# Spreading a mixture-of-experts kernel's indirect row DMAs over its expert rounds, one per step

## What is computed

```python
x = x + _L0_conv_ref(_ln_c(x), ...)       # kq, v, softmax(kq kq^T), out projection, per image of 256 points
t = _to_tokens(x)
t = t + _L0_ffn_ref(_ln_t(t), ...)
# _L0_ffn_ref, flat = the 2048 normalised tokens of 64 values
logits = flat @ router_w.T
topk_probs, topk_idx = jax.lax.top_k(jax.nn.softmax(logits, axis=-1), 2)     # of 8 experts
gates = ...                                # the two probabilities over their sum
h = silu(flat @ w1[e].T) * (flat @ w3[e].T)                                  # 682 values
out = sum over the token's two experts of gate * (h @ w2[e].T)
```

## Time and profile before

| | us |
|---|---|
| Median of 3 runs | 175.12 |
| Lowest, highest | 175.03, 176.37 |
| Span of the profiled execution, first to last instruction | 238.2 |
| PE, DVE, ACT, POOL busy in it | 166.9, 99.7, 70.8, 85.7 |

### The profile page before, as it was taken

The page is one execution under the profiler, slowest core; times in us unless marked ns, Lnnn a source line. Parts: engine busy times, 40 slices in busy tenths (PEclk is TensorE's granted clock), DMA queues, the critical chain, the costliest instruction groups (busy, mean ns, idle before and its releaser), DMA issues.

```text
span 238.2 us, 4880 instructions
## 1 busy us (share of the span) xinstructions
PE 166.9 (70%) x1682; PEld 139.1 (58%) x1682; DVE 99.7 (42%) x372; ACT 70.8 (30%) x141; POOL 85.7 (36%) x114
## 2 busy tenths in 40 slices
PE   3595957428683069589494994958949697895683
PEld 2364836307452068588393983948839597783543
DVE  2557568255583037584222433223232344342230
ACT  2377433013310034224232142222422323333101
POOL 2963577723277700603205033060230604142400
PEclk9999586555578559979799598895997979798579
DMA  6990000184570229652958075390661600000053
GB/s 185 322 297 20 11 25 22 31 267 151 159 290 23 50 81 328 216 210 46 364 169 313 3 240 196 88 346 4 203 228 42 266 10 14 11 15 11 17 176 91
DMA packets 19893, 33.00 MB, mean 139 GB/s; under 512 B 7691, under 2 KB 13100, under 8 KB 19868
## 3 DMA queue, kind: packets, MB, share of 16 engines
q1 hardware_dynamic: 16732, 29.55, 37.8%
q0 software_dynamic: 2272, 2.35, 3.0%
q10 hardware_dynamic: 864, 0.79, 1.0%
HBM read 25.55 MB, written 7.13 MB: 137 GB/s over the span
## 4 chain that ended last, share of the span: by engine, by line
issue 48%; POOL 21%; PE 11%; DVE 8%; DMA 3%; another core or an unknown queue 3%; ACT 3%; POOLq 1%; SPq 0%; ACTq 0%; DVEq 0%
POOL ys L370 15%; POOL xs L361 5%; PE psum L925 3%; PE psum L914 2%; ACT xn L426 2%; DMA y_in<-ys 2%; DVE rows L595 1%; PE psum L894 1%; PE psum L1103 1%; PE psum L885 1%; DMA ys<-y_out,y_row 1%; DMA proj<-projections 1%; DVE index L606 1%; DVE neg_max L584 1%
## 5 line engine op out<-in xcount | busy, mean ns | idle before, releaser
L370 POOL DMA_INDIRECT ys<-y_out,y_row x39 | 37.4, 960 | 104.0 <-DVE y_out L839 95.2
L827 DVE TENSOR_TENSOR hid<-psum,act_sb 128x512 f32<-128x512 f32 (+1 forms) x50 | 33.4, 676 | 88.9 <-ACT act_sb L504 61.6
L1031 PE MATMUL psum<-x_cols,weights 64*128 64x128 f32 x390 | 52.9, 286 | 13.9 <-issue 12.1
L1031 PEld LDWEIGHTS psum<-x_cols,weights 64*128 64x128 f32 x390 | 47.6, 193 | 19.4 <-issue 15.8
L1033 PE MATMUL psum<-x_cols,weights 64*128 64x128 f32 x390 | 53.1, 286 | 0.9 <-issue 0.9
L504 ACT ACTIVATE act_sb<-psum 128x512 f32<-128x512 f32 (+1 forms) x50 | 28.7, 586 | 70.0 <-remote 42.4
L1033 PEld LDWEIGHTS psum<-x_cols,weights 64*128 64x128 f32 x390 | 47.7, 193 | 1.1 <-issue 1.1
L1059 PE MATMUL psum<-hid,weights 128*64 128x128 f32 x468 | 42.8, 357 | 2.1 <-issue 1.1
L1059 PEld LDWEIGHTS psum<-hid,weights 128*64 128x64 f32 x468 | 39.3, 189 | 4.8 <-issue 2.7
L361 POOL DMA_INDIRECT xs<-xrows,pos x32 | 31.6, 987 | 12.9 <-issue 8.9
L1037 PE MATMUL psum<-x_cols,weights 64*106 64x128 f32 x78 | 8.7, 349 | 23.1 <-ACT act_sb L504 18.4
(11 more groups left out here) (148 smaller groups left out, 189.9 us busy)
## 6 DMA issues: line engine op xcount, KB each, us to landing
weights<-experts SPq DMA_DIRECT2D x39, 565.0 KB
xs<-zeros SPq DMA_DIRECT2D x4, 1040.0 KB, 11.1
x_in<-xs SPq DMA_DIRECT2D x39, 32.5 KB
ys<-y_out,y_row POOLq DMA_INDIRECT x39
xs<-xrows,pos POOLq DMA_INDIRECT x32
y_in<-ys ACTq DMA_DIRECT2D x2, 256.0 KB, 4.5
y_in<-ys SPq DMA_DIRECT2D x2, 256.0 KB, 4.3
x_sb<-x_tok SPq DMA_DIRECT2D x1, 384.0 KB, 3.4
```

What stands on the lines that cost most here:

```text
L370: nc.gpsimd.indirect_dma_start(ys, bass.IndirectOffsetOnAxis(ap=y_row[:, j:j + 1], axis=0), y_out[:, i % RING, h, :], None).then_inc(y_sca ...
L827: nc.vector.tensor_tensor(live(i, hid[:, i % 2, s, :]), live(i, H3_BANK[g % 3]), live(i, act_sb[:, g % 3, :]), ALU.mult).then_inc(hid_done, 1)
L1031: first_ = nc.tensor.matmul(H1_BANK[g % 2][:, src], weights[0:C, slot, P * s:P * (s + 1)], x_cols[0:C, i % 2, src], start=True, stop=True)
```

## The change

```diff
             add_biases(3)
             pool.wait_ge(tables_made, TABLES)
 
+            def pace(n):
+                if n < 8:
+                    i, k, points = n // 4, n % 4, (1, 3, 5, STEPS)
+                elif n < 28:
+                    i, k, points = 2 + (n - 8) // 5, (n - 8) % 5, (1, 2, 3, 5, STEPS)
+                elif n < 44:
+                    i, k, points = 6 + (n - 28) // 4, (n - 28) % 4, (1, 3, 5, STEPS)
+                else:
+                    return
+                if points[k] < STEPS:
+                    pool.wait_ge(silu_done, STEPS * i + points[k] + 1)
+                else:
+                    pool.wait_ge(hid_used, i + 1)
+
             t_deviation(0)
             for p in range(PAIRS):
                 for at in range(TPP * K_TOP):
-                    if p == 0 and at == TPP * K_TOP - 2 or p == 2 and at == K_TOP:
-                        t_deviation(p + 1)
+                    if p == 0 and at == TPP * K_TOP - 2:
+                        t_deviation(1)
+                    if p == PAIRS - 1:
+                        pace(at)
                     scatter_row(p, at)
-                if p == 1:
-                    t_deviation(2)
+                if p in (1, 2):
+                    t_deviation(p + 1)
             for j in range(NS):
+                pace(TPP * K_TOP + j)
                 scatter_result(j)
```

## The result

The changed kernel takes 180.2 us in the median (179.25 to 181.21, 4 runs) against 175.75 us (175.03 to 178.52, 4 runs) for the kernel before: the ratio is 1.029, 95% interval 1.022 to 1.035. It is slower by some 4.5 to 5 us, outside the range that was forecast.

The account below looks back on a forecast made before the run. PE bounds the kernel by the totals, bursts of indirect DMAs the profiled execution, but timed runs go nearly without those stalls. 175.1 + 0 (pair 2) + 0 (pair 3) + 0 (end) - 0.2 (bursts) = 174.9 us, range 171.5 to 178.0.

Parts of the forecast that it names:

- The timed runs without stalls: Whole kernel: timed runs hold at most some 4 us of the profile's stalls; rebuilt time 173.6 to 177.9 us.
- Pair 2's rows: Eight rows in one go from 55.25, pair 3's deviation 1.2 us later but hidden: value 0, perhaps up to 1 us gained.
- Results from round 2 on, and the end: Paced result scatters and the last results: no wait for the y_out ring, cost 0, with 0.4 us of cover at the end.
- Pair 3's rows: Rows spread over rounds 0 and 1, feeding round 4's weights: margin 2.0 to -0.4 us, taken as no loss.
- the row has landed, SP issues the row loads: Eighth row's landing after round 1: 2.13 us on empty queues, about 5.9 beside weights; SP not free before 92.9.
- from there to the issue of the weights: SP's row loads, 1.9 us, and table reads, 2.75 us, ahead of issuing round 4's weights.
- the weights stream and land: Round 4's weights from issue to landing: 8.6 us, read off a DMA share between 111.6 and 120.
- start of round 4, if nothing is late: When PE wants round 4's weights: 108.1, or 18.8 us after the end of round 1, with rounds of 9.4 us.
- C: Rival at round 4: eighth row late and SP's row loads slow, so PE waits for weights; some 3 us, 178 us; chance 0.22.
- B: Rival: timed runs keep part of the stalls and single scatters win some 3.5 us back, 171.6 us; chance 0.24.
- D: Rival at POOL: it reaches paced points late, so scatters still go in runs; ends at 174.9 us; shares chance 0.54.
- the sign that the results stand singly: Sign of being right: in the changed profile pair 3's rows and the results stand singly at their steps.

Follow-up runs that it names:

- e1: Changed kernel with pair 3's rows sent back to back, not paced, and results still paced: 175.27 us, ratio 0.9995.
- e3: Changed kernel with nothing paced, leaving only pair 2's rows in one go with pair 3's deviation behind them: 175.23 us, ratio 1.0003.
- e0: The kernel before, unchanged, profiled a second time: span 175.2 us, 177.66 us for that execution; 19 others had a median of 176.18 us.
- e6: Changed kernel with only pair 3's eighth row moved, 1.35 us sooner, right behind the seventh: 179.15 us, ratio 1.015.
- e7: Changed kernel with only pair 3's eighth row moved, 3.6 us later, to step 1 of round 2: 182.0 us, ratio 1.027.
- e10: Kernel before with one SP wait added ahead of round 4's row loads, for the silu of step 3 of round 2: 179.12 us, ratio 1.021.
- e9: Changed kernel with pair 3's seventh and eighth rows at steps 3 and 4 of round 1: 176.79 us, ratio 1.003.
- e8: Changed kernel loading only the first half of the columns of round 3's weights: 176.09 us, ratio 1.0004.
- e2: Changed kernel with the results not paced and pair 3's rows still paced: 179.27 us, ratio 1.026.
- e4: Changed kernel with round 4's weights issued ahead of SP's wait for pair 3's rows, the row loads behind it: 184.5 us, no ratio.

## Why the prediction was wrong

**The timed runs without stalls: right.** The sum gave 173.6 to 177.9 us for the kernel without the first profile's stalls; the profiles that have none span 173.4 (e1, e3) and 175.2 us (e0). Part of that is luck, since its terms err in both directions: by the sum round 0 starts at 61.8 us, takes 11.4 and a later round 9.4; in e0 it starts at 63.5, takes 10.2 and a later round 9.0. The sum also took clock off for stretches in which PE was idle. The reasons beside it were not right. I tied the stalls to POOL's bursts and to the profiler; e0 has profiler and bursts, and no stall. What stalled that one execution stays open, and no run here shows whether back-pressure had a part in it.

**Pair 2's rows: right.** Worth nothing (e3).

**Results from round 2 on, and the end: right.** Cost 0 (e1).

**Pair 3's rows: the step that failed.** The path was named in full: eighth row, SP's wait, row loads, table reads, weights of round 4, PE. The place where it ended, "a margin of 2.0 to -0.4 us: I take no loss", did not hold; it was -2.3 us. By its terms, from the end of round 1:

| term | forecast, us | changed kernel, us |
|---|---|---|
| the row has landed, SP issues the row loads | 2.1 to 5.9, at least 3.6 | 5.75 |
| from there to the issue of the weights | 4.65 | 4.3 |
| the weights stream and land | 8.6 | 10.2 |
| start of round 4, if nothing is late | 18.8 | 18.0 |
| margin | 2.0 to -0.4 | -2.3 |

The landing came out at the bound that I had called the nearer one, and I then took the other. The largest error is the stream: 8.6 us was read off a window's DMA share (111.6 to 120), which says how long the engines were busy, and not when the last of four loads had landed. Issue to PE's release took 10.2 us in the changed kernel, 10.7 and 10.8 in e6 and e7, 10.5 in e10, 9.9 in e9. The round was 9.4 us by my sum and is 9.0: 0.8 us of margin that was not there.

**What the sum did not have at all** is the clock behind the wait: 1.6 us at the start of round 4 on top of the 2.3. And PE's one wait is not the whole: the next `x_in` is late too (3.75 us of DVE's time at 104.94), since SP has little slack in a round and its queue carries row loads behind weights.

**The rivals.** C was the case, in its mechanism and its place, with a price of 3 us where 4.5 to 5 was right and its slow SP issue not needed (1.90 us, as ever). B, that single scatters win time back, falls: with and without pacing the results the time is the same (e1, e3). D was in part the case: POOL kept up with the rows of pair 3, as the prediction worked out, but not with the results at steps 1, 2 and 3 of rounds 2 to 5, 16 of which still go in runs of four. So the sign that the results stand singly was not met there, and it cost nothing (e1, e3).

On pair 3's rows the Trainium skill (DMA: Bandwidth & Descriptors, Queues, rings and completion order), by which a DMA engine takes turns between its queues packet by packet, had the direction right: e8 shows the row's lateness going with the weight stream. Turns alone are not what the trace shows, though: the eighth row's packets moved within 1.0 us, and 3.9 us passed before the first of them. No run here shows what held them.

## What to carry to other kernels

Before a transfer is moved from a quiet stretch to a busy one, follow the wait that it feeds through the queue of the engine that waits, up to the first consumer, and take each landing from issue to release beside a full stream. If the sum from the nearer bounds ends at no margin, forecast the loss, and add the clock that PE may give up after a wait. And where a profile's span is far from the timed median, profile the same kernel again before reading its stalls.

## What was not expected of the hardware

The clock behind a wait is not certain. In e6 PE waited 3.36 us at the start of round 4, longer than in the changed kernel, and was granted 1.00 right behind it, where the changed kernel had 0.52 after 2.31 us, e2 0.54 after 2.59, e10 0.56 after 2.46 and e7 0.71 after 3.42 (window of e6):

```profile
105.15:108.50 3.35, 3.35 (x48) 3.06 (x50) 1.53 (x4) 1.44 (x3) 0.00 (x0) 1.00 0.99 372
```

One execution of the same program spanned 238.2 us and another 175.2 us, with the same bursts of indirect DMAs; in the first alone PE, ACT and SP stood still beside POOL's bursts.

An indirect DMA of 128 rows lands 2.13 us after it starts on empty queues and 5.32 to 6.81 us after beside a weight stream (the changed kernel, e6, e9), and sending it 5.0 us later (e6 to e7) moves what waits for it by only 1.6 us. A plain load of 32.5 KB behind a round of weights on its own queue took 7 us from issue to its consumer's release (e4).
